# Second FFN: shared plus routed weights summed once per expert, kept in DRAM and fetched per segment

## The reference, cut to what matters

```python
x = x + A @ (layernorm(x) * W)                     # third adj stage
h = relu(flat @ Wi.T + bi)                         # second FFN, HID = 256
for l in range(2):
    shared = h @ Ws[l].T + bs[l]
    routed = h @ Wr[l, e].T + br[l, e]             # e = route_id of the token's segment
    h = relu(shared + routed + h)
out = h @ Wo.T + bo
```

## Time and profile before

| what | before |
|---|---|
| median of 3 runs | 1025.38 us (1025.15 to 1025.98) |
| span of the profiled execution | 1013.7 us |
| around the span, taken as median less span | 11.7 us |
| PE busy | 993.1 us, 98% |
| LDWEIGHTS busy | 529.6 us, 52% |
| DVE busy | 416.6 us, 41% |
| ACT busy | 310.8 us, 31% |
| POOL busy | 179.0 us, 18% |
| chain that ended last | PE 93%, ACT 3%, DVE, issue and DMA 1% each |
| DMA | 220.57 MB, 218 GB/s over the span |

### The profile page before, as it was taken

How to read it: one execution, slowest core, us unless ns; L and a number is a source line. 1 busy time by engine, 2 the same in 40 slices (tenths; PEclk the granted TensorE clock), 3 DMA queues, 4 the chain that set the end, 5 groups by cost and what they waited for, 6 DMA issues and landing times.

```text
span 1013.7 us, 12482 instructions
## 1 busy us (share of the span) xinstructions
PE 993.1 (98%) x3618; PEld 529.6 (52%) x3618; DVE 416.6 (41%) x1443; ACT 310.8 (31%) x601; POOL 179.0 (18%) x216
## 2 busy tenths in 40 slices
PE   8999999999999999999997999989999999999997
PEld 4555555555555444444443588734545445454554
DVE  6323223323313344334434156562453424535266
ACT  4644645645541000000001254241312223122231
POOL 4110010010010122121222144551011010110101
PEclk9999999999999999999999899989999999999999
DMA  9995675366104788888854743167464564645300
GB/s 363 421 416 196 258 319 241 133 290 277 56 0 167 296 331 301 309 306 305 323 207 170 266 120 112 31 215 280 166 258 178 188 239 166 257 179 187 156 1 22
DMA packets 41664, 220.57 MB, mean 218 GB/s; under 512 B 6644, under 2 KB 22712, under 8 KB 29430
## 3 DMA queue, kind: packets, MB, share of 16 engines
q1 hardware_dynamic: 38454, 215.21, 55.2%
q0 software_dynamic: 2864, 4.39, 1.3%
q10 hardware_dynamic: 272, 0.13, 0.0%
HBM read 210.29 MB, written 11.62 MB: 219 GB/s over the span
## 4 chain that ended last, share of the span: by engine, by line
PE 93%; ACT 3%; DVE 1%; issue 1%; DMA 1%; DVEq 0%; POOL 0%; SPq 0%; ACTq 0%; POOLq 0%
PE PA L1822 22%; PE PA L1573 22%; PE PA L1593 22%; PE O L1768 3%; PE O L1886 3%; ACT U L682 3%; PE O L1642 3%; PE PA L1551 2%; PE T L1906 2%; PE T L1895 1%; PE SR L1886 1%; PE SM L1886 1%; PE O L1614 1%; PE O L1604 1%; PE O L1863 1%
## 5 line engine op out<-in xcount | busy, mean ns | idle before, releaser
L1822 PE MATMUL PA<-ring,S 128*128 128x512 f32 x512 | 236.0, 602 | 3.4 <-issue 3.4
L1593 PE MATMUL PA<-ring,S 128*128 128x512 f32 x512 | 229.8, 595 | 1.2 <-DMA ring<-in_adj_cols 1.2
L1573 PE MATMUL PA<-ring,U 128*128 128x512 f32 x512 | 226.7, 595 | 0.0
L1573 PEld LDWEIGHTS PA<-ring,U 128*128 128x128 f32 x512 | 94.8, 190 | 106.6 <-issue 106.5
L1593 PEld LDWEIGHTS PA<-ring,S 128*128 128x128 f32 x512 | 95.4, 190 | 102.4 <-issue 98.7
L1822 PEld LDWEIGHTS PA<-ring,S 128*128 128x128 f32 x512 | 92.9, 192 | 103.8 <-issue 100.5
L602 ACT ACTIVATE work<-ring 128x2048 int8<-128x2048 f32 x64 | 122.2, 1910 | 9.0 <-issue 4.7
L1429 DVE TENSOR_TENSOR U<-ring,work 128x512 f32<-128x512 f32 x112 | 81.8, 735 | 89.4 <-PE SR L1886 45.5
L750 ACT ACTIVATE work<-T,work 128x64 f32<-128x64 f32 x112 | 29.0, 310 | 66.8 <-PE T L1895 54.2
L847 POOL DMA_INDIRECT disp_d<-work x32 | 31.9, 997 | 96.4 <-DVE work L1263 89.1
L859 POOL DMA_INDIRECT y_d<-R,work x40 | 39.3, 983 | 51.1 <-DVE R L1331 41.1
(11 more groups left out here) (271 smaller groups left out, 1086.4 us busy)
## 6 DMA issues: line engine op xcount, KB each, us to landing
ring<-in_adj_cols SPq DMA_DIRECT2D x52, 2048.0 KB, 9.3
ring<-in_adjT_cols SPq DMA_DIRECT2D x32, 2048.0 KB, 7.2
ring<-in_adj_cols SPq DMA_DIRECT2D x8, 1024.0 KB, 13.6
work<-in_w SPq DMA_DIRECT2D x16, 256.0 KB, 2.8
ring<-in_Wr SPq DMA_DIRECT2D x1, 4096.0 KB, 12.1
ring<-in_Wr SPq DMA_DIRECT2D x2, 2048.0 KB, 13.3
disp_d<-U SPq DMA_DIRECT2D x4, 650.0 KB, 19.4
work<-disp_d SPq DMA_DIRECT2D x8, 325.0 KB, 3.7
```

What stands on the lines that cost most here:

```text
L1573: mm = nc.tensor.matmul(out_T[:, :], X[:, t * D:(t + 1) * D], ring[slot][t // HT][:, (t % HT) * BW:(t % HT + 1) * BW], start=n == 0, stop= ...
L1593: mm = nc.tensor.matmul(PA[k % 2][:, :], S[:, t * D:(t + 1) * D], ring[slot][t // HT][:, (t % HT) * BW:(t % HT + 1) * BW], start=t == 0, s ...
L1822: mm = nc.tensor.matmul(PA[slot][:, :], S[:, t * D:(t + 1) * D], ring[1][t // HT][:, (t % HT) * BW:(t % HT + 1) * BW], start=t == 0, stop= ...
```

## The change

The shared weights (plus the identity) are added to `Wr` in place, four experts at a time, by eight DVE instructions of 128 x 2048 in the expert stage; SP stores each slice to a new DRAM tensor `w_d`. In the third stage SP reads the segment's expert and fetches the summed 256 KB from `w_d` into one of 16 buffers, which lie where the second half of `Wr` was; PE waits for the four loads of a group. `stage_w` and its waits are gone. `Wr` is loaded in quarters, each once layer 2 has read that quarter of `ring[0]`. `WsT` is loaded at the start of layer 2 over weights that are used up by then, and gets its identity there, after the tail of the third block.

```diff
+        w_d = nc.dram_tensor("w_d", [L2 * E2, P, KH * DH], F32).ap()
...
-        WS = 4
-        wst = [U[:, KH * BW + KH * DH * i:KH * BW + KH * DH * (i + 1)] for i in range(WS)]
+        wst = [ring[0][1][:, KH * DH * i:KH * DH * (i + 1)] for i in range(L2 * SB)]
+        SLICE = 4
+        NS = L2 * E2 // SLICE
...
+        STORED = ((), (), (0,), (1,), (2, 3), (4,), (5, 6), (7,))
...
                 sp.dma_start(gbc, A["gate_b_bc"]).then_inc(s_wts2, 16)
+                sp.dma_start(w_s, A["WsT"]).then_inc(s_wself, 16)
...
-            sp.wait_ge(s_agg2, NB)
-            sp.wait_ge(s_sc, 16 * (NT - BT))
-            sp.dma_start(ring[0][0][:, :], A["Wr"][0]).then_inc(s_ring[0][0], 16)
-            sp.dma_start(ring[0][1][:, 0:QUART], A["Wr"][1, :, 0:QUART]).then_inc(s_ring[0][2], 16)
+            for n, q in enumerate(ORDER2):
+                if n < 3:
+                    sp.wait_ge(s_quart2, (NB - 1) * 3 + n + 1)
+                else:
+                    sp.wait_ge(s_agg2, NB)
+                at = q % 2 * QUART
+                sp.dma_start(ring[0][q // 2][:, at:at + QUART], A["Wr"][q // 2, :, at:at + QUART]).then_inc(s_ring[0][q], 16)
             sp.wait_ge(s_sc, 16 * NT)
...
                 load_weights(e, e % 2)
+                for i in STORED[e]:
+                    sp.wait_ge(s_pre, i + 1)
+                    alone(sp)
+                    sp.dma_start(w_d[SLICE * i:SLICE * (i + 1)].rearrange("e p n -> p e n"), slice_of(i)).then_inc(s_wkept, 16)
...
-            for b in range(1, NB):
-                for q in range(4):
-                    if q < 3:
-                        sp.wait_ge(s_quart3, (b - 1) * 3 + q + 1)
-                    else:
-                        sp.wait_ge(s_agg3, b)
+            def load_group(k, g):
+
+                if k > 1:
+                    sp.wait_ge(s_wu, (k - 2) * (L2 * SB) + (g + 1) * SH)
                     alone(sp)
-                    load_quarter(sp, adjT, b, 1, q)
+                for n in range(g * SH, (g + 1) * SH):
+                    l, s = n // SB, n % SB
+                    e = sp.value_load(route_sb[0:1, ds((k - 1) * SB + s, 1)], min_val=0, max_val=E2 - 1)
+                    sp.dma_start(wst[n], w_d[ds(e + l * E2, 1)].rearrange("o p n -> (o p) n")).then_inc(s_wg[g], 16)
...
+            sp.wait_ge(s_wts3, 16 * len(F2_INPUTS))
+            sp.wait_ge(s_wkept, 16 * NS)
+            for g in range(NG):
+                load_group(1, g)
+            for q in range(4):
+                refill3(1, q)
+            for b in range(2, NB + 1):
+                if b < NB:
+                    refill3(b, 0)
+                load_group(b, 0)
+                if b < NB:
+                    refill3(b, 1)
+                load_group(b, 1)
+                load_group(b, 2)
+                if b < NB:
+                    refill3(b, 2)
+                load_group(b, 3)
+                if b < NB:
+                    refill3(b, 3)
...
+            def self_weights():
+
+                dve.wait_ge(s_wself, 16)
+                alone(dve)
+                for l in range(L2):
+                    for kk in range(KH):
+                        diag = w_s[:, (l * KH + kk) * DH + kk * P:(l * KH + kk) * DH + (kk + 1) * P]
+                        nc.vector.tensor_tensor(diag, diag, ident[:, :], ALU.add)
...
+            def add_self(i):
+
+                l = i // (NS // L2)
+                if i % 2 == 0:
+                    dve.wait_ge(s_ring[0][i // 2], 16 * 8)
+                    alone(dve)
+                shared = w_s[:, l * KH * DH:(l + 1) * KH * DH].unsqueeze(1).to_broadcast([P, SLICE, KH * DH])
+                nc.vector.tensor_tensor(slice_of(i), slice_of(i), shared, ALU.add).then_inc(s_pre, 1)
...
             for e in range(2):
                 tags(e, e)
+            for i in range(4):
+                add_self(i)
             for e in range(E1):
                 expert(e, e % 2, e // 2 if e >= 2 else None)
                 if e + 2 < E1:
                     tags(e + 2, e % 2)
+                if e + 4 < NS:
+                    add_self(e + 4)
...
-                for n in range(10, L2 * SB):
-                    stage_w(NB, n)
...
-                for n in range(2, L2 * SB):
-                    stage_w(k, n)
-                    if n in RAW_AT:
-                        raw_rows(k, RAW_AT.index(n))
-                raw_rows(k, NG - 1)
...
+                for g in range(NG):
+                    raw_rows(k, g)
...
+                pe.wait_ge(s_wg[g], 16 * SH * k)
                 for pair in range(SH // 2):
...
-                    pe.wait_ge(s_wst, (k - 1) * (L2 * SB) + n0 + 2)
```

More of the change, by code:

```diff
@@ L111, in build @@
         tri = sb("tri", [P, P], BF16)
-        W_io = sb("W_io", [P, DH])
-        W_s1 = sb("W_s1", [P, DH])
-        W_us = sb("W_us", [P, KH, 2 * D])
+        W = sb("W", [P, 2 * DH + KH * 2 * D])
+        W_io = W[:, 0:DH]
+        W_s1 = W[:, DH:2 * DH]
+        W_us = W[:, 2 * DH:].rearrange("p (k c) -> p k c", k=KH, c=2 * D)
+        w_s = W[:, 0:L2 * KH * DH]
         b_us = sb("b_us", [P, 2 * D])
@@ L187, in build @@
         at += DH
-        w_s = part(at, L2 * KH * DH)
-        at += L2 * KH * DH
         w_o = part(at, KH * D)
@@ L221, in build @@
         b_last = small[:, 48:48 + L2 * KH * SB].rearrange("p (lm s) -> p lm s", lm=L2 * KH, s=SB)
-        last_w = [ring[1][0][:, KH * DH * i:KH * DH * (i + 1)] for i in range(L2 * SB)]
-        raw = [U[:, KH * BW + KH * DH * WS + BW * i:KH * BW + KH * DH * WS + BW * (i + 1)] for i in range(2)]
+        raw = [U[:, KH * BW + BW * i:KH * BW + BW * (i + 1)] for i in range(2)]
         mv3 = e_rows[0][:, 0:2 * NT]
@@ L372, in build @@
         s_h0 = sem("s_h0")
-        s_wst = sem("s_wst")
+        s_wself = sem("s_wself")
+        s_pre = sem("s_pre")
+        s_wkept = sem("s_wkept")
+        s_wg = [sem(f"s_wg{g}") for g in range(NG)]
         s_wu = sem("s_wu")
@@ L1114, in fold_weights @@
                 dve.wait_ge(s_wprod, 1)
[L1115 to L1116 removed]
+                nc.vector.tensor_copy(W_s1, SR[:, 0:DH])
+                nc.vector.tensor_copy(W_io, O[0][:, 0:DH])
                 nc.vector.tensor_copy(W_us[:, :, 0:D], tiles(O[1][:, 0:2 * D], KH))
@@ L1283, in step2 @@
                 route(k)
+            def self_weights():
[5 more added lines that the diff above has]
+                        nc.vector.tensor_tensor(diag, diag, ident[:, :], ALU.add)
             for k in range(1, NB - 1):
                 step2(k, k % 2, (k + 1) // 2)
+                if k == 3:
+                    self_weights()
             for k in (NB - 1, NB):
@@ L1414, in _ @@
                         last.then_inc(s_hid, 1)
[L1417 to L1430, removed]
             def raw_rows(k, g):
-                dve.wait_ge(s_wu, (k - 1) * (L2 * SB) + (g + 1) * SH + WS)
+                dve.wait_ge(s_wu, (k - 1) * (L2 * SB) + (g + 1) * SH)
                 alone(dve)
@@ L1487, in inner_step3 @@
                 stats(lambda t: x3[:, t * D:(t + 1) * D], BT).then_inc(s_mv4, 1)
-                for n in range(2):
-                    stage_w(k, n)
                 dve.wait_ge(s_rstd4, k)
@@ L1603, in self_rows @@
                         pe.wait_ge(s_u2u, (k - 1) * 2 + t // 2 + 1)
-                    mm = nc.tensor.matmul(O[t // 2][:, t % 2 * DH:(t % 2 + 1) * DH], hT[k % 2][:, t * P:(t + 1) * P], W_s1[:, :], start=True, stop=True)
+                    mm = nc.tensor.matmul(O[t // 2][:, t % 2 * DH:(t % 2 + 1) * DH], hT[k % 2][:, t * P:(t + 1) * P], W_s1, start=True, stop=True)
                     if t % 2 == 1:
@@ L1613, in out_rows @@
                         pe.wait_ge(s_zpre, k * 2 + t // 2 + 1)
-                    nc.tensor.matmul(O[t // 2][:, t % 2 * DH:(t % 2 + 1) * DH], aT[:, t * P:(t + 1) * P], W_io[:, :], start=True, stop=True).then_inc(s_o1, 1)
+                    nc.tensor.matmul(O[t // 2][:, t % 2 * DH:(t % 2 + 1) * DH], aT[:, t * P:(t + 1) * P], W_io, start=True, stop=True).then_inc(s_o1, 1)
             def turn_h(k):
@@ L1877, in routed @@
                         pe.wait_ge(s_lv, g - SB // SH + 1)
-                weights = wst if k < NB else last_w
+                pe.wait_ge(s_wg[g], 16 * SH * k)
                 for pair in range(SH // 2):
@@ L1887, in routed @@
                                                   src[:, kk * BW + s * SEG:kk * BW + (s + 1) * SEG],
-                                                  weights[(n0 + c) % len(weights)][:, kk * DH:(kk + 1) * DH], start=kk == 0, stop=kk == KH - 1)
+                                                  wst[n0 + c][:, kk * DH:(kk + 1) * DH], start=kk == 0, stop=kk == KH - 1)
                             if kk == KH - 1:
```

17 lines of the change are left out of this document (11 added, 6 removed).

## The result

The changed kernel takes **1019.93 us** (median of 4 runs, 1018.65 to 1022.09) against 1025.28 us of the kernel before in the same session: a ratio of 0.9949, 95% interval 0.9935 to 0.9963. It is faster by 0.5%, and the prediction (no change, 1025.4 us, range 1024.0 to 1029.5) was wrong.

A forecast was written before the change was run, and what follows sets the result against it. TensorE, busy for 98% of the span, was taken to bound the kernel, not the relieved VectorE. Every term came to 0, so the forecast stayed at 1025.4 us, range 1024.0 to 1029.5, with no change at 0.72.

The forecast's parts named there:

- The step that failed: Whole kernel: the 11.7 us between profile span and median time stay unchanged, so a change of span changes the median equally.
- The wide adds: Expert stage, VectorE: eight adds of 2.3 us each fit in its holes; cost 0, at worst 0.5 us.
- The removed adds: Third stage: 78 us of VectorE adds lie beside TensorE's work; removing them gives 0, at most 0.2 us.
- rival (3): Third stage: TensorE's busy time hides semaphore waits behind routed groups; removing half gains 2.7 us, giving 1022.7; chance 0.08.
- The tail: After 988 us: removing the last block's sixteen adds moves nothing that ends last; 0, at most a gain of 0.8 us.
- `Wr` earlier: Between layer 2 and the experts: loading these weights earlier leaves the start of the transposes at 570.72 unchanged; 0.
- The stores: Expert stage: 8 MB stored ahead of experts' rows still lets them land in time; cost 0, 1.0 us at 265 GB/s.
- Rival (2): Expert stage: stores delay the rows of experts 5 and 7 below 277 GB/s; 5.6 us at 220, giving 1031.0; chance 0.10.
- The sixteen loads by SP: Third stage, each block: 0.8 to 1.2 us per load on SP, 13 to 19 us in all, hidden; cost 0.
- rival (1): Third stage, first block: SP's register loads delay the refill from 1.51 us each; 4.6 us at 1.8, giving 1030.0; chance 0.09.

The follow-up runs named there:

- the first trace: Kernel before, unchanged: its profile recorded ahead of the prediction, with a span of 1013.7 us, while its timed runs had a median of 1025.38 us.
- the changed kernel, again: The changed kernel, unchanged, measured and profiled a second time: 1021.37 us, ratio 0.9961 to the kernel before; span of the profile 1019.4 us.
- second trace of before: Kernel before, unchanged, measured and profiled again: 1025.06 us, ratio 1.0002; span of the profile 1024.2 us.

## Why the prediction was wrong

**The step that failed** is the one that it made in passing: "I take the 11.7 us between span and median (1025.38) as unchanged". In all 166 executions of this study that have a span beside their time, 1.7 to 3.7 us lie around it, 2.1 in the median; the other 10 us were lost *inside* the timed executions, in the expert stage and the passage behind it, which the first trace shows at their full pace. So every sum was made against an execution without the waits that the change removes.

**The wide adds** were sized rightly (2.3 us forecast, 2.29 measured) and hidden as forecast. Their term of the sum, a cost of 0 with at worst 0.5 us, is where the waits would have had to stand: wide instructions in these places, beside the early load of `Wr` that gave nothing, made the kernel before 1025.37 - 1020.72 = 4.65 us faster. The prediction even saw that "POOL's scatters start a little later". What it lacked was a reason why this could be a gain: its bounds for this part had no end below zero, and in the first trace scatters did nothing to TensorE.

**The removed adds.** The bound of 0.2 us for the third stage was too narrow: the products take 325.53 to 325.55 us in the traces of the changed kernel that fetch from `w_d`, 326.27 to 326.31 in those built on the kernel before, a gain of 0.75 us. It is not where rival (3) looked; the pieces of 2.77 and 2.58 us are the same in both. The chain shows one group of four transposes in each block that takes 0.55 us before,

```profile
853.08 0.55 PE T L1895 x4
```

and 0.44 us after (the changed kernel, again), which is 7 x 0.11 = 0.77 us:

```profile
848.71 0.44 PE T L1932 x4
```

VectorE's timelines of the same two traces show what the transposes wait for. In the kernel before, the copy of the sums that they turn stands behind an add and ends at 852.92, 0.06 us ahead of their start at 852.98; in the changed kernel it ends at 848.13, 0.41 us ahead of theirs at 848.54.

```profile
851.63 0.69 DVE L1429 TENSOR_TENSOR U<-ring,work 128x512 f32<-128x512 f32 x1 [1.24 <-PE SM L1886]
852.24 0.68 DVE L1439 COPY U<-SM 128x512 f32<-128x512 f32 x1
```

```profile
847.44 0.69 DVE L1490 COPY U<-SM 128x512 f32<-128x512 f32 x1 [3.96 <-PE SM L1923]
```

Without the stores the products take 326.47 us, but only because the first block takes 31.50 in place of 30.60; its other seven are as short as in the changed kernel.

So rival (3), waits hidden in busy time, was right in kind and a fourth of its size. The tail gave 0 as forecast: the two copies of sums now start at 1003.26 and 1004.99, each right behind its own products, and the time from the last product to the end is 24.84 us (24.71 and 24.82 before). The changed kernel without adds, 0.18% [0.05, 0.30] faster than before, bounds what all parts but the adds are worth; the 0.75 us lie within it.

**`Wr` earlier**: 0 forecast, ratio 1.0008 measured alone. Right; the transposes start at 570.09.

**The stores**: 0 forecast. Right: without them the time stays (0.9957 against 0.9949 and 0.9961 with them). Rival (2) didn't happen; the steps stay at 9.66 us with the stores running.

**The sixteen loads by SP**: 0.8 to 1.2 us each forecast, 1.17 measured, far from the 1.51 of rival (1); the DMA share came to 0.80 where 0.75 was forecast. A refill lands in 9.5 us in the median instead of 7.2, unseen by TensorE:

```profile
ring<-in_adjT_cols SPq DMA_DIRECT2D x25, 2048.0 KB, 9.5
```

So the change does what it was forecast to do, and gains 0.75 us by it. The rest of its 5 us is a side effect of where it put eight wide instructions, and three more of them, behind experts 4 to 6, give about as much again: 1015.48 us, the fastest version here that leaves nothing out.

## What to carry to other kernels

Hold the span of a profile against the time of the runs first: where the gap is larger than another profile of the same program family shows (here 11.7 us against some 2), the trace is not of a typical execution, and a second one is worth more than any sum. In a trace, look for two engines that start at the same instant although they wait for different things, long after the producer named has ended: there the signal was late, not the work. And when a change wins, put its parts in alone; instructions that compute nothing can show that a gain belongs to their place and not to their purpose.

## What was not expected of the hardware

- Five scatters that POOL issues 1.27 us apart can hold up TensorE's signals to VectorE and ScalarE by 0.4 to 3.3 us, and by 3.8 us in the last expert (second trace of before). A wait of some 1.5 us in the third (it lasts 2.39 to 2.58 us in place of 0.97) frees the signals, and two scatters close together did not hold them up in experts 1 to 6.
- Not every execution shows it: the first trace has five close scatters and no hold-up, and in one session the 23 runs of before lay at 1021.5 us in the median, 2.5 to 4 us below the others. What in the chip holds the signals is open. In the first trace every landing of a scatter is recorded (640 of 640 events between 560 and 690 us), in the second only 208 are; the traces without hold-ups lack events too, so this alone doesn't decide. Whether the recording itself has a part in it was not tried.
- One 128x2048 add on VectorE stops a scatter on POOL until it is done (2.39 us in place of 0.97); with sixteen 128x128 products in a row one lasted 2.13 us, so short instructions without pauses leave POOL little room as well.
